# Scan, projection and attention in one block; the lowest parts of x formed by GpSimd; earlier scales and an earlier bias product

## The reference

```python
x = x + scan_layer(layernorm(x))       # state space scan, 16 states per channel
x = x + ffn(layernorm(x))              # sqrt((x@cos(theta))**2 + (x@sin(phi))**2)
x = x + attention(layernorm(x))        # 16 heads of 16 channels, rotary q and k
x = x + ffn(layernorm(x))              # the same weights as above
```

## Time and profile before

| | us |
|---|---|
| median of 3 runs (lowest, highest) | 3500.74 (3498.16, 3501.07) |
| profiled execution, its time | 3502.53 |
| profiled execution, its span | 3500.6 |
| busy in the span: PE, DVE, ACT, POOL | 3336.5, 3256.8, 2721.5, 829.3 |

### The profile page before, as it was taken

One profiled execution on the slowest core, in us unless ns is written; L12 is line 12 of the kernel. 1 busy time (PEld: TensorE's weight loads), 2 busy tenths in 40 slices (PEclk: granted clock), 3 DMA queues, 4 the chain that ended last, 5 costly groups with the idle time before them and its releaser, 6 DMA issues.

```text
span 3500.6 us, 59749 instructions
## 1 busy us (share of the span) xinstructions
PE 3336.5 (95%) x22826; PEld 1197.2 (34%) x22852; DVE 3256.8 (93%) x4952; ACT 2721.5 (78%) x4999; POOL 829.3 (24%) x707
## 2 busy tenths in 40 slices
PE   6788888987999999999999999999999999999999
PEld 3222222442333333333333333333333333333334
DVE  7999998469999999999999999999999999999943
ACT  6766665664888888888888888888888888888865
POOL 3899997672000000000000000000000000000004
PEclk9999999997999999999999999999999999999999
DMA  2000001042020202202020202012020202020011
GB/s 65 1 10 0 0 1 48 16 155 36 8 33 6 33 11 30 30 10 33 6 33 8 33 6 33 14 28 32 7 33 6 35 7 33 6 33 6 8 55 48
DMA packets 53678, 87.11 MB, mean 25 GB/s; under 512 B 13200, under 2 KB 40464, under 8 KB 49232
## 3 DMA queue, kind: packets, MB, share of 16 engines
q1 hardware_dynamic: 53200, 82.77, 12.6%
q10 hardware_dynamic: 192, 0.52, 0.1%
HBM read 53.37 MB, written 21.23 MB: 21 GB/s over the span
## 4 chain that ended last, share of the span: by engine, by line
PE 79%; DVE 10%; issue 4%; POOL 3%; ACT 1%; DVEq 0%; POOLq 0%; DMA 0%; SPq 0%; ACTq 0%
PE att_banks L1485 29%; PE att_banks L1442 16%; PE att_banks L1437 15%; PE att_banks L1400 11%; DVE arena L998 5%; DVE arena L968 3%; PE att_banks L1398 2%; PE decay L553 2%; PE att_banks L553 2%; POOL arena L1127 1%; DVE arena L1654 1%; DVE arena L979 1%; PE att_banks L1507 1%; POOL arena L1133 1%; POOL arena L1101 0%
## 5 line engine op out<-in xcount | busy, mean ns | idle before, releaser
L1637 DVE TENSOR_REDUCE arena<-att_banks 128x1 f32<-128x512 f32 x4032 | 2503.8, 683 | 19.1 <-PE att_banks L1400 15.5
L1612 ACT ACTIVATE arena<-att_banks 128x512 f32<-128x512 f32 x4096 | 2114.6, 603 | 417.4 <-PE att_banks L1437 409.5
L1437 PE MATMUL att_banks<-arena 64*128 64x512 bf16 x4032 | 1248.0, 380 | 0.0
L1442 PE MATMUL att_banks<-arena 35*128 35x512 bf16 x4032 | 1208.8, 379 | 0.3 <-ACT arena L1612 0.2
L1485 PE MATMUL att_banks<-arena 128*32 128x512 f32 x8192 | 1090.9, 605 | 0.0
L1398 PE MATMUL att_banks<-arena 64*128 64x512 bf16 x2048 | 790.6, 388 | 31.8 <-DVE arena L1654 20.1
L1400 PE MATMUL att_banks<-arena 64*128 64x512 bf16 x2048 | 788.8, 387 | 0.6 <-DVE arena L1637 0.6
L1437 PEld LDWEIGHTS att_banks<-arena 64*128 64x128 bf16 x4032 | 376.3, 93 | 392.6 <-PE att_banks L1442 8.4
L1400 PEld LDWEIGHTS att_banks<-arena 64*128 64x128 bf16 x2048 | 188.4, 93 | 796.0 <-DVE arena L1637 791.8
L1442 PEld LDWEIGHTS att_banks<-arena 35*128 35x128 bf16 x4032 | 358.2, 94 | 157.3 <-ACT arena L1612 9.2
L1364 POOL TENSOR_TENSOR arena<-arena 64x512 f32<-64x512 f32 x64 | 81.0, 1265 | 1189.7 <-DMA arena<-arena 1155.3
(11 more groups left out here) (148 smaller groups left out, 1748.9 us busy)
## 6 DMA issues: line engine op xcount, KB each, us to landing
arena<-qk_parts SPq DMA_DIRECT2D x242, 128.0 KB, 7.1
qk_parts<-arena SPq DMA_DIRECT2D x32, 384.0 KB, 2.6
arena<-arena SPq DMA_DIRECT2D x63, 128.0 KB, 2.3
x_res<-in_x SPq DMA_DIRECT2D x8, 512.0 KB, 8.9
arena<-in_trig SPq DMA_DIRECT2D x2, 2048.0 KB, 8.6
arena<-qk_parts SPq DMA_DIRECT2D x64, 64.0 KB, 10.7
att_t<-arena SPq DMA_DIRECT2D x128, 32.0 KB
arena<-att_t SPq DMA_DIRECT2D x8, 512.0 KB, 5.6
```

What stands on the lines that cost most here:

```text
L1437: return nc.tensor.matmul(sc[:, (4 * t + j) % SB, :], k, q, start=(j == 1), stop=(j != 1))
L1442: return nc.tensor.matmul(sc[:, (4 * t + j) % SB, :], k, q, start=(j != 1), stop=(j == 1))
L1612: nc.scalar.activation(prob[:, t % PBUF, j * CH:(j + 1) * CH], sc[:, n % SB, :], ACT.Exp, scale=SCALE).then_inc(exp_done, 1)
L1637: nc.vector.tensor_reduce(part_max[:, b % 2, u // NC, u % NC:u % NC + 1], mx[:, unit_bank(b, u), :], AXX, ALU.max).then_inc(dve_read, 1)
```

## The change

- The lowest parts of x in the norm stage are formed by POOL instead of DVE, one chunk behind `what_hi_leaves`.
- `scan_to_projection` and `attention` share one block. Each returns its five engine programs, and these are run one after the other in it, so the engines no longer meet between them. All of PSUM is one tensor, `mem.banks`. Waits on single semaphores stand in place of the meeting: PE's first two groups of attention products wait for the last reads of their banks, and ACT's first loads for the stores of the parts.
- DVE computes the scale of FFN unit 0 ahead of the last scan tile. ACT copies the turned unit 0 ahead of normalising unit 1. The products of unit u go to `decay[:, u % 2]`, and PE waits for one scan tile less before the products of unit 0.
- DVE instead of ACT normalises projection chunks 0 and 1, at its own FFN units 12 and 13.
- The product of value bias and Wo is made behind PE's FFN unit 9, in `yb`, and DVE adds it at unit 12.

The diff without changes of indentation, cut:

```diff
@@ norm_and_project, gpsimd
+                def low(i):
+                    pool.wait_ge(mid_ready, i + 1)
+                    nc.gpsimd.tensor_tensor(mem.xp[:, 2, :, cols(i)], rest[:, i % 2], mem.xp[:, 1, :, cols(i)],
+                                            ALU.subtract).then_inc(lo_ready, 1)
                 for i in range(NC):
                     what_hi_leaves(i)
+                    if i >= 1:
+                        low(i - 1)
+                low(NC - 1)
@@ norm_and_project, vector
-                def low(i):
-                    dve.wait_ge(mid_ready, i + 1)
-                    nc.vector.tensor_tensor(mem.xp[:, 2, :, cols(i)], rest[:, i % 2], mem.xp[:, 1, :, cols(i)],
-                                            ALU.subtract).then_inc(lo_ready, 1)
...
-                    if i >= 1:
-                        low(i - 1)
...
-                low(NC - 1)
@@ FfnUnits.act_start
         self.act_normalise(act, 0)
+        self.act_copy_turned(act, 0)
         self.act_normalise(act, 1)
         self.act_deviations(act, 2)
-        self.act_copy_turned(act, 0)
@@ scan_to_projection
-                         ri=lambda u: decay[:, (u + 1) % 2, :].rearrange("p (k a d) -> p k a d", k=UT, a=2))
+                     ri=lambda u: decay[:, u % 2, :].rearrange("p (k a d) -> p k a d", k=UT, a=2))
@@ tensor
+        def out_bias():
+            pe.wait_ge(out_loaded, 48)
+            pe.wait_ge(x_added, NSC * DH)
+            for h in range(DH):
+                last = nc.tensor.matmul(yb[:, 0:D], b_v[:, h, :], mem.w_o[:, h, :], start=(h == 0), stop=(h == DH - 1))
+            last.then_inc(bias_ready, 1)
...
-                pe.wait_ge(scan_done, NT_SCAN)
+        pe.wait_ge(scan_done, NT_SCAN - 1)
                 units.pe_products(pe, 0)
                 scan_tile(NT_SCAN - 1)
+        pe.wait_ge(scan_done, NT_SCAN)
                 units.pe_products(pe, 1)
                 turn_y(NSC * DH, NT_SCAN)
                 for u in range(2, NU_F - 1):
                     units.pe_products(pe, u)
+            if u == EARLY_U + 1:
+                out_bias()
...
-                    pe.wait_ge(xn_ready, i + 1)
+            if i < 2:
+                pe.wait_ge(xn_by_dve, i + 1)
+            else:
+                pe.wait_ge(xn_by_act, i - 1)
...
-                pe.wait_ge(x_added, NSC * DH)
+        pe.wait_ge(bias_added, 1)
                 turn(0)
                 units.pe_products(pe, NU_F - 1)
...
-                pe.wait_ge(out_loaded, 48)
-                pe.wait_ge(v_read, NC)
-                for h in range(DH):
-                    last = nc.tensor.matmul(vb[:, 0, :], b_v[:, h, :], mem.w_o[:, h, :], start=(h == 0),
-                                            stop=(h == DH - 1))
-                last.then_inc(bias_ready, 1)
@@ scalar
-                    if u >= NU_F - 2:
-                        normalise(u - NU_F + 2)
@@ vector
                     if n in (NT_SCAN - 3, NT_SCAN - 2):
                         unit_stats(n - NT_SCAN + 3)
+            if n == NT_SCAN - 2:
+                units.dve_scale(dve, 0)
...
+        def normalise(i):
+            for k in range(TPC):
+                t = i * TPC + k
+                last = nc.vector.tensor_scalar(xn[:, i, k, :], mem.x[:, t, :], mem.mv[:, t, 0:1], mem.rstd[:, t, :],
+                                               ALU.subtract, ALU.mult)
+            last.then_inc(xn_by_dve, 1)
...
-                units.dve_scale(dve, 0)
                 units.dve_scale(dve, 1)
...
                     if u == EARLY_U + 4:
                         scale_and_shift(early, 1)
+                normalise(0)
+                dve.wait_ge(bias_ready, 1)
+                nc.vector.tensor_tensor(mem.b_o[:, 0, :], yb[:, 0:D], mem.b_o[:, 0, :], ALU.add).then_inc(bias_added, 1)
+            if u == EARLY_U + 5:
+                normalise(1)
...
-                dve.wait_ge(bias_ready, 1)
-                nc.vector.tensor_tensor(mem.b_o[:, 0, :], vb[:, 0, :], mem.b_o[:, 0, :], ALU.add).then_inc(bias_added, 1)
@@ attention
-            return banks[:, g % 2 * WIDE:(g % 2 + 1) * WIDE, :]
+        return banks[:, (g + 1) % 2 * WIDE:((g + 1) % 2 + 1) * WIDE, :]
@@ tensor
                     m, t = g // QT, g % QT
+            if g == 0:
+                pe.wait_ge(mem.values_read, NC)
+            if g == 1:
+                pe.wait_ge(mem.pairs_read, NC * 2 * DH)
@@ scalar
+        for parts in mem.parts_stored:
+            act.wait_ge(parts, 16 * NC)
                 load_rows(act, k_rows, 0, 1, K_TWIN, 0, first_loaded, cols=slice(QH, S))
@@ hybrid_kernel
-        scan_to_projection(nc, mem, io)
-        attention(nc, mem, io, out)
+        middle, last = scan_to_projection(nc, mem, io, ctx), attention(nc, mem, io, out, ctx)
+        with nc.Block() as block:
+            @block.sync
+            def _(sp):
+                for part in (middle, last):
+                    part[0](sp)
...
```

More of the change, by code:

```diff
@@ L1752, in hybrid_kernel, with _ @@
         norm_and_project(nc, mem, io)
-        scan_to_projection(nc, mem, io)
-        attention(nc, mem, io, out)
+        mem.banks = ctx.enter_context(nc.psum_tensor("banks", [P, 8, CH], F32))
+        middle, last = scan_to_projection(nc, mem, io, ctx), attention(nc, mem, io, out, ctx)
[4 more added lines that the diff above has]
+                    part[0](sp)
+            @block.tensor
+            def _(pe):
+                for part in (middle, last):
+                    part[1](pe)
+            @block.scalar
+            def _(act):
+                for part in (middle, last):
+                    part[2](act)
+            @block.vector
+            def _(dve):
+                for part in (middle, last):
+                    part[3](dve)
+            @block.gpsimd
+            def _(pool):
+                for part in (middle, last):
+                    part[4](pool)
 def rope_tables():
```

1816 lines of the change are left out of this document (902 added, 914 removed).

## The result

The changed kernel takes 3488.87 us as the median of 9 runs (3485.59 to 3490.24), the kernel before 3500.74 in the same comparison (3498.16 to 3504.87). The ratio is 0.9963, with a 95% interval of 0.9954 to 0.9973: 11.9 us faster, predicted 13.0. In the profiled executions the spans are 3486.7 and 3500.6 us, 13.9 apart, so the terms of the prediction can be checked one by one in the two traces.

What follows compares the result with a forecast made beforehand. PE was taken as full in FFN, projection and attention, leaving some 180 us between them to change. Terms summed to -13.0 us: 3502.5 to 3489.5 profiled, less 1.8 for the median, 3487.7 us; range 3480.5 to 3494.

Steps and rivals of the forecast that it cites:

- Norm stage: Start of the kernel: moving the lowest parts to POOL adds work that must take turns, +1.2 us, bounds -0.4 to +3.2.
- The turns: POOL and DVE: instructions such as DVE's with two SBUF inputs hold each other off; whoever asks first gets the whole.
- the 41.0 us: Joint POOL and DVE work from 38 us that must take turns, so the norm stage can't end before 79.0 us.
- Scan end to FFN: Last scan tile to full PE: unit 0's early scale starts FFN unit 1's products sooner, -5.3 us, bounds -6 to -2.
- Bias product: In the FFN: the value bias and Wo product now stands in the full PE, +0.9 us.
- late scales: In the FFN: DVE's added work delays unit 15's scale, mostly taken up by ACT, +0.3 us, bounds 0 and +1.5.
- FFN end to projection: Unit 14's products to chunk 0's values: earlier normalising removes PE waits and values run warm, -10.1 us; if cold, -8.1.
- Merge: Way into the attention: the first product waits for a transfer, so removing the engines' meeting gives 0.
- Case 1: Norm stage: no turns, POOL's new work fits into gaps, -5.2 instead of +1.2 us; 3481.3 us, chance 0.12.
- Case 2: FFN and projection starts: PE stays cold, terms -2 and -8.1 us; 3493.0 us, chance 0.16.
- Case 3: Attention's first block: the clock comes back later after the shifted start, making it slower; 3508 us, chance 0.04.
- Case 4: Way into the attention: the last transfer lands sooner without the meeting, at most 1.94 us won; 3485.8 us, chance 0.06.

Runs made afterwards that it cites:

- e_low_dve: Changed kernel with the lowest parts of x formed by DVE again: profiled span 3488.4 us against 3486.7.
- e_no_low2: Changed kernel with no lowest parts formed and no fill, the middle part read again in their place: profiled span 3480.4 us against 3486.7.
- the square: Four profiled runs, attention's early loads late or early, without/with engines meeting before attention: late 3486.7 (changed kernel)/3486.3 us, early 3475.3/3485.6 us.
- the pair shown above: Timelines of the changed kernel and of it with projection and attention as two blocks again, same norm stage: spans 3486.7 and 3486.3 us.

## Why the prediction was right, step by step

The time, 3488.9 for 3487.7, lies in the range, and the mechanisms are in the main those of the prediction. Part of the agreement is luck: the medians lie 11.9 apart and the two traces 13.9, with 13.0 between them, and at the projection's start the clock stayed up in this trace as forecast, which it did in seven traces of twelve. By its own steps:

- **Norm stage, +1.2.** Measured +0.3. The turns are real (2.99 and 2.85 for 1.38, the last `normalise` at 58.4), and taking the subtractions away gives 6.4 us. The term came out 0.9 high: the stage ended at 78.46, under the floor of 79.0, so the 41.0 us were a little too many, but eight traces of this stage scatter by 1.6 us, so the sign of the term isn't settled. That the small `normalise` overlap in part, as the lower bound had it, fits but was not measured by itself. The Trainium skill ("SBUF — State Buffer", section "Who interferes with whom") was named for the rule, and the traces agree; they also show a fill by POOL, which reads nothing, holding DVE's `normalise` for 6 us.
- **Scan end to FFN, -5.3.** Measured -5.7 behind the last scan, and 0.3 of it paid ahead of it (the scale runs from 593.02 to 593.33). Undoing it alone costs 5.7. The half unit took 1.72, as forecast for a warm PE, and 3.75 with the late scale. PE's longest pause there was 1.6 us, not the 1.2 of the prediction.
- **Bias product, +0.9; late scales, +0.3.** Measured 0.86 and 0: PE has no pause in the FFN, so ACT took up the delay whole.
- **FFN end to projection, -10.1.** Measured -9.9, but the reason was only in part right. The prediction put the 5.49 and the 5.38 of the kernel before down to PE's pauses and let them go with the pauses. The experiments show the clock falling or staying behind the same pause: behind 3.16 us it was 0.69 once and 1.00 once, and behind 2.1 us the values took 3.69 us in seven traces and 5.38 in five. So 5.3 us are the edit's own; 3.0 are how the clock fell in one execution of before; and the last 1.6 came because it stayed up in the profiled execution of after. "The clock fell in the trace only after longer ones" was a rule made from one execution, and its other bound, -8.1, was nearly as likely. This may be part of why the medians lie 11.9 apart and the spans 13.9; that was not tried.
- **Merge, 0.** Measured 0.1, and the same 89.6 us with two blocks: the transfer bounds it. The prediction stopped there. It didn't ask what the merge would be worth once that transfer was early, which is 10.3 us in the span and 10.6 at the join.
- **Rivals.** Case 1 is refuted by `e_low_dve` and `e_no_low2`. Case 2 did not come as a whole, but single pieces of it did: the values at 5.38 us in five traces, and the sum of tile 126 at 3.5 to 3.6 in three. Case 3 did not come: from the first attention product to the end it takes 2719.3 us, before 2719.2. Case 4 is refuted by the square. The swap of the banks and ACT's new order ahead of the FFN, both priced at nothing, were not undone by themselves.

## What to carry to other kernels

When a wait is removed and nothing moves, look for the wait that ends just beside it, and remove both before judging either: here either alone is worth 0 to 1 us and would have been given up, and the pair gave 11. An instruction moved to an idle engine is free only if the two engines can run it beside each other; count the joint work of the pair, not the idle time of the one. And where a forecast leans on a clock that fell in one trace, price the piece at both clocks, since the same code behind the same pause ran at either.

## What the runs showed of the hardware

POOL's MEMSET of 128x8192 bf16, 6.92 us, held four DVE instructions with one tensor input (7.33 for 1.38), though it has no input at all. PE's granted clock differed between runs of the same instructions behind the same pause (0.69 and 1.00 behind 3.16 us; 16 products in 3.69 and 5.38 us behind 2.1), and where the fall met the first tiles of the scan, whose bound is DVE, the scan took 1.6 to 2.3 us longer than in the changed kernel. The Trainium skill ("TensorE: Matmul & The Clock Gate", section "What's actually happening") says that the moment at which the clock changes varies from run to run, with the start of a kernel as its example; these traces show it for falls in mid-kernel. The second chunk of x arrived up to 2.5 us sooner or later (7.5 to 10.0 us), and in the pair shown above 1.3 of 2.1 us reached the end of the norm stage.
